# Six staging slots, later loads and projections dealt out over slots, in layers 2 and 3 of a four-layer block on one core

## The reference, cut to what matters

```
def layer2(x, c, context):                      # x: (4, 1024, 256), 16 heads of 16
    shift_a, scale_a, gate_a, shift_m, scale_m, gate_m = split(silu(c) @ W_mod + b_mod, 6)
    q, k, v = split((ln(x) * (1 + scale_a) + shift_a) @ W_qkv + b_qkv, 3)
    x = x + gate_a * (softmax(q k^T / 4) v @ W_proj + b_proj)
    x = x + (softmax(q_c k_c^T / 4) v_c @ W_cproj + b_cproj)   # k_c, v_c from 77 context rows
    return x + gate_m * (gelu((ln(x) * (1 + scale_m) + shift_m) @ W_mlp1 + b_mlp1) @ W_mlp2 + b_mlp2)

def layer3(x, context, c):
    return x + (softmax(q_3 k_3^T / 4) v_3 @ Wp + bp)
```

## Time and profile before

| | |
|---|---|
| median of 3 runs | 3452.23 us (3444.96 to 3454.8) |
| the profiled execution | 3451.98 us |
| its span, first to last instruction | 3450.2 us, mean granted TensorE clock 0.950 |
| TensorE busy (products) | 3162.4 us, 92% of the span |
| VectorE busy | 1824.0 us, 53% |
| ScalarE busy | 1467.0 us, 43% |
| GpSimd busy | 256.9 us, 7% |

### The profile page before, as it was taken

One profiled execution on the slowest core, in us unless ns is written; L12 is line 12 of the kernel. 1 busy time (PEld: TensorE's weight loads), 2 busy tenths in 40 slices (PEclk: granted clock), 3 DMA queues, 4 the chain that ended last, 5 costly groups with the idle time before them and its releaser, 6 DMA issues.

```text
span 3450.2 us, 52900 instructions
## 1 busy us (share of the span) xinstructions
PE 3162.4 (92%) x21156; PEld 1867.7 (54%) x21156; DVE 1824.0 (53%) x3812; ACT 1467.0 (43%) x2645; POOL 256.9 (7%) x278
## 2 busy tenths in 40 slices
PE   6899999999889999999389989999999999999987
PEld 3555665656566666666244445454454544554464
DVE  4876554563411322322278865757756577556433
ACT  0343535444322222221136645565455565565533
POOL 1100010001100000000100001001110101001010
PEclk9898999999898999999789999999999999999998
DMA  5200000002100000000321020001200000000000
GB/s 168 91 1 6 8 21 1 8 21 68 45 12 11 0 1 1 1 0 1 135 77 35 26 74 25 11 24 44 86 13 22 28 29 25 13 28 25 7 1 13
DMA packets 78713, 104.39 MB, mean 30 GB/s; under 512 B 18688, under 2 KB 52208, under 8 KB 78204
## 3 DMA queue, kind: packets, MB, share of 16 engines
q1 hardware_dynamic: 78468, 100.93, 8.9%
HBM read 72.05 MB, written 28.86 MB: 29 GB/s over the span
## 4 chain that ended last, share of the span: by engine, by line
PE 80%; DVE 10%; DMA 3%; ACT 3%; issue 2%; SPq 1%; POOL 1%; DVEq 0%; ACTq 0%; POOLq 0%
PE ps L978 73%; PE ps L1193 3%; DVE max_halves L1684 2%; DMA k_parts<-qk_parts 1%; PE ps L1320 1%; PE ps L1184 1%; DVE row_max_cross L1850 1%; DMA q_parts<-qk_parts 1%; PE ps L1172 1%; ACT big L2028 1%; ACT probs L2087 1%; DVE bn_stats L1720 1%; DMA q_blocks<-q_parts 1%; DVE xn_tok L1756 1%; SPq L879 1%
## 5 line engine op out<-in xcount | busy, mean ns | idle before, releaser
L2028 ACT ACTIVATE big<-ps 128x512 f32<-128x512 f32 x1280 | 693.7, 595 | 639.5 <-PE ps L978 638.6
L1684 DVE TENSOR_REDUCE max_halves<-ps 128x1 f32<-128x512 f32 x1024 | 650.4, 684 | 222.1 <-PE ps L978 219.4
L978 PE MATMUL ps<-k_groups,q_blocks 32*128 32x512 f32 x2048 | 451.6, 463 | 71.0 <-DVE qk_parts L1819 34.8
L978 PE MATMUL ps<-q_blocks,k_groups 32*128 32x512 f32 x2048 | 422.5, 466 | 3.3 <-DVE qk_parts L1819 2.0
L978 PE MATMUL ps<-big,probs 128*32 128x512 f32 (+2 forms) x3280 | 397.1, 531 | 5.0 <-ACT o_T L2003 3.8
L978 PE MATMUL ps<-weights_mlp,big 128*128 128x256 f32 (+1 forms) x1248 | 333.4, 419 | 2.5 <-ACT big L2099 2.5
L978 PEld LDWEIGHTS ps<-q_blocks,k_groups 32*128 32x128 f32 x2048 | 178.4, 185 | 286.1 <-issue 273.9
L978 PEld LDWEIGHTS ps<-weights_mlp,big 128*128 128x128 f32 x1248 | 233.7, 190 | 83.9 <-issue 58.0
L978 PEld LDWEIGHTS ps<-k_groups,q_blocks 32*128 32x128 f32 x2048 | 197.6, 189 | 120.9 <-DVE qk_parts L1819 39.0
L1726 DVE TENSOR_TENSOR x_tok<-ps,x_tok 128x512 f32<-128x512 f32 x112 | 77.3, 691 | 307.6 <-PE ps L978 307.4
L2087 ACT ACTIVATE probs<-ps 77x512 f32<-77x512 f32 x384 | 196.5, 592 | 96.8 <-PE ps L978 96.5
(11 more groups left out here) (233 smaller groups left out, 3913.6 us busy)
## 6 DMA issues: line engine op xcount, KB each, us to landing
q_blocks<-q_parts SPq DMA_DIRECT2D x64, 256.0 KB
q_parts<-qk_parts SPq DMA_DIRECT2D x48, 256.0 KB
k_parts<-qk_parts SPq DMA_DIRECT2D x32, 256.0 KB
k_groups<-k_parts SPq DMA_DIRECT2D x16, 512.0 KB
weights_mlp<-in_L_xcond_mlp_W SPq DMA_DIRECT2D x5, 1024.0 KB, 5.4
weights_mlp<-in_L_xcond_W_mlp SPq DMA_DIRECT2D x5, 1024.0 KB, 5.6
x_tok<-in_x SPq DMA_DIRECT2D x4, 1024.0 KB, 9.6
out_y<-x_tok SPq DMA_DIRECT2D x8, 512.0 KB, 2.9
```

The costliest lines, as they stand in the source:

```text
L978: return pe.matmul(out, lhsT, rhs, start=first, stop=last)
L1684: dve.tensor_reduce(NMP[:, e, j, qt, hf:hf + 1], PS[:, bank, :], AX.X, ALU.max, negate=True).then_inc(R.frees(key), 1)
L2028: act.activation(PB[:, score % 2, j, :], PS[:, R.bank(key), :], ACT.Exp, scale=SCALE).then_inc(R.frees(key), 1)
```

## The change: what it does

1. Item 0's staging gets four more slots (`EARLY`, in a part of `big` that cross-attention and the MLP use later). Projections 0 and 1 use the two old slots, 2 to 5 the four new ones, and from projection 6 on the two old slots alternate. Six semaphores count the writes. `parts_before(n)` is the projection whose writes n waits for: n - 6 for projections 6 and 7, n - 2 later.
2. `p_tokens` puts the v product of each half of the heads behind that half's four projections, not behind all eight.
3. `open_to` deals the projections out. Item 0's first four are free; its projections 4 to 7 wait for slots -8, -4, 0 and 4. Projection n of a later item b waits for slot 6 + 6n of item b - 1.
4. Item 0's loads are placed only when three block loads have been placed. SP issues the weights (W1, two biases, the four cross-attention weights) behind the third block load, and these four weights are taken into the same function.
5. Item 0's gates are placed 60 us after their loads on the planner's clock, not 14 us. The planner's estimate for a block load is 12 us for the first and 6 us for a later one, at least 3 us after the one before.

```diff
+        EARLY = BIG[:, 12288:16384].rearrange("p (s x n) -> p s x n", s=4, x=2)
+
+        def parts_at(n):
+            return EARLY[:, n - STAGES] if STAGES <= n < STAGES + 4 else STG[:, n % STAGES].bitcast(F32)
...
-                done = sum(48 if k[2] == 0 else 32 for k in self.parted[n % STAGES:n + 1:STAGES])
-                return self.part_out[n % STAGES], done
+                done = sum(48 if k[2] == 0 else 32 for k in self.parted[n % 6:n + 1:6])
+                return self.part_out[n % 6], done
+
+            def parts_before(self, n):
+
+                return self.parted[n - 6 if n < 6 + STAGES else n - STAGES]
...
-                return out + [("qk", b, m, a, hf) for m in range(KT) for a, hf in ((1, 0), (1, 1), (0, 0), (0, 1))] + [("v", b, m) for m in range(KT)]
+                for m in range(KT):
+                    out += [("qk", b, m, a, hf) for a, hf in ((1, 0), (1, 1), (0, 0), (0, 1))] + [("v", b, m)]
+                return out
...
-                    out.append((("gate", what, b), [("load", what, b)], 14.0))
+                    out.append((("gate", what, b), [("load", what, b)], 60.0 if R.split and not b else 14.0))
...
                 if kind == "qk" and R.split:
-                    return True
+                    n = 4 * tok[2] + (tok[4] if tok[3] else NH + tok[4])
+                    return t >= (tok[1] - 1) * R.total + 6 + 6 * n if tok[1] else n < 4 or t >= 4 * n - 24
...
-                    if item in loads and item[2] == 0.0 and all(k in ended for k in item[1]):
+                    if item in loads and item[2] == 0.0 and all(k in ended for k in item[1]) and (not R.split or state["ld"] >= Q_BLOCKS):
...
-                    ended["ld", state["ld"] - 1] = state["now"] + 5.0
+                    ended["ld", state["ld"] - 1] = max(state["now"] + (12.0 if state["ld"] == 1 else 6.0), ended.get(("ld", state["ld"] - 2), 0.0) + 3.0)
...
-            for item in list(loads):
+            for item in list(loads) if not R.split else ():
...
+                def weights():
+                    sp.dma_start(W1, rowsview(io[pre + ("mlp_W1" if R.l == 0 else "W_mlp1")])).then_inc(R.w1_in, 16)
+                    if R.l == 2:
+                        sp.dma_start(BX, bcast(io[L2 + "b_cproj"])).then_inc(R.w1_in, 16)
+                        sp.dma_start(B3, bcast(io[L3 + "bp"])).then_inc(R.w1_in, 16)
+                        sp.dma_start(Wcq, rowsview(io[L2 + "W_qc"])).then_inc(cross_w, 16)
...
+                if not R.split:
+                    weights()
...
+                    if tok == ("ld", Q_BLOCKS - 1):
+                        weights()
...
-                            if n >= STAGES:
-                                dve.wait_ge(*R.parts_landed(*R.parted[n - STAGES]))
+                            if n >= 6:
+                                dve.wait_ge(*R.parts_landed(*R.parts_before(n)))
...
-                            if n >= STAGES:
-                                act.wait_ge(*R.parts_landed(*R.parted[n - STAGES]))
-                            act.activation(STG[:, n % STAGES, 0, :], PS[:, R.bank(tok), 0:w], ACT.Identity, bias=QB[:, 3 * a, m:m + 1]).then_inc(R.part_hi, 1)
+                            if n >= 6:
+                                act.wait_ge(*R.parts_landed(*R.parts_before(n)))
+                            act.activation(parts_at(n)[:, 0, :].bitcast(F32R), PS[:, R.bank(tok), 0:w], ACT.Identity, bias=QB[:, 3 * a, m:m + 1]).then_inc(R.part_hi, 1)
```

More of the change, by code:

```diff
@@ L322, in __init__ @@
                     self.part_hi, self.nm_f, self.nm_h = sems(name, "part_hi max_f32 max_hi")
-                    self.part_out = sems(name, "parts_out_0 parts_out_1")
+                    self.part_out = sems(name, "parts_out_0 parts_out_1 parts_out_2 parts_out_3 parts_out_4 parts_out_5")
                     self.q_in = sems(name, "q_block_in_0 q_block_in_1 q_block_in_2")
@@ L689, in overlapped @@
                 for item in list(loads):
-                    if item in loads and all(k in ended for k in item[1]) and max(ended[k] for k in item[1]) + item[2] <= now:
+                    if item in loads and item[1] and all(k in ended for k in item[1]) and max(ended[k] for k in item[1]) + item[2] <= now:
                         loads.remove(item)
@@ L719, in overlapped @@
                 else:
-                    waits = [f[0] for f in found] + [max(ended[k] for k in item[1]) + item[2] for item in loads if all(k in ended for k in item[1])]
+                    waits = [f[0] for f in found] + [max(ended[k] for k in item[1]) + item[2] for item in loads if item[1] and all(k in ended for k in item[1])]
                     assert waits, (R.name, state, [s[h] for h, s in zip(heads, streams) if h < len(s)], loads)
@@ L860, in gate @@
                     sp.dma_start(dst, MODd[b:b + 1, base + chunk * D:base + (chunk + 1) * D].broadcast_to([P, D])).then_inc(done, 16)
[L862 to L865, removed]
+                def weights():
[4 more added lines that the diff above has]
+                        sp.dma_start(Wcq, rowsview(io[L2 + "W_qc"])).then_inc(cross_w, 16)
+                        sp.dma_start(Wco, rowsview(io[L2 + "W_cproj"])).then_inc(cross_w, 16)
+                        sp.dma_start(Wcq3, rowsview(io[L3 + "Wq"])).then_inc(cross_w, 16)
+                        sp.dma_start(Wco3, rowsview(io[L3 + "Wp"])).then_inc(cross_w, 16)
+                if not R.split:
+                    weights()
                 for tok in R.order:
@@ L878, in region_sp @@
                             dst = KPd[b, m, :, x, :, hf * HALF:(hf + 1) * HALF] if a else QPd[b, m, hf, :, x]
-                            sp.dma_start(dst, STG[:, n % STAGES, part, :].bitcast(F32)).then_inc(R.part_out[n % STAGES], 16)
+                            sp.dma_start(dst, parts_at(n)[:, part, :]).then_inc(R.part_out[n % 6], 16)
                     if tok[0] == "ld":
@@ L967, in _ @@
             sp.dma_start(BV, bcast(io[L2 + "b_qkv"][2 * D:3 * D])).then_inc(bv_in, 16)
[L968 to L971, removed]
             region_sp(L2R)
@@ L1813, in region_dve @@
                             n = R.parted.index(tok[1:])
-                            parts = STG[:, n % STAGES]
+                            parts = parts_at(n)
                             dve.wait_ge(*R.full(tok))
-                            if n >= STAGES:
-                                dve.wait_ge(*R.parts_landed(*R.parted[n - STAGES]))
+                            if n >= 6:
+                                dve.wait_ge(*R.parts_landed(*R.parts_before(n)))
                             dve.wait_ge(R.part_hi, n + 1)
-                            dve.scalar_tensor_tensor(parts[:, 1, :], PS[:, R.bank(tok), 0:w], QB[:, 3 * a, m:m + 1], parts[:, 0, :].bitcast(F32), ALU.add, ALU.subtract).then_inc(R.frees(tok), 1)
+                            dve.scalar_tensor_tensor(parts[:, 1, :].bitcast(F32R), PS[:, R.bank(tok), 0:w], QB[:, 3 * a, m:m + 1], parts[:, 0, :], ALU.add, ALU.subtract).then_inc(R.frees(tok), 1)
                         elif hf:
```

## The result

The changed kernel takes 3430.62 us (median of 4 runs, 3422.96 to 3432.92) and the kernel before, run beside it, 3453.52 us: 0.9938 of it, with an interval of [0.9917, 0.9959]. It is faster by 23 us, where 42 were forecast. The profiled execution took 3432.92 us, with a span of 3431.1 us.

The account below looks back on a forecast made before the run. A chain of write, landing, evacuation and bank bounds the start, TensorE the rest of layers 2 and 3. -49 + 10 - 6 + 2 + 1 = -42 from 3452 gives 3410 us, range 3396 to 3438.

Parts of the forecast that it names:

- first exponential: Start of layers 2 and 3: item 0's first exponential at 1720 us instead of 1769.05, -49 us.
- moved work: Four projections, a v pair and item 1's transposes move into slots bound by TensorE: net +10 us (8 to 13).
- gates: Item 0's gate products on POOL near slot 8, between two row-maximum steps: taken as +1 us, up to 8 if colliding.
- block loads: Item 0's slots: q writes ahead of block 8's load cost 3 us, block 4 gains 1.03: +2 us (0 to 12).
- dealing out: Items 1 to 3, a projection every six slots: waits in the two later clusters go, -6 us (0 to -12).
- estimate of about 4 us that stood beside the sum: Each block load behind a projection's three q writes pays about 4 us if both use the same four DMA engines.
- the 3 us that should have come back as waits: TensorE's waits for projections between 1764 and 1804.6 us lose their cause; 3 us counted as gain against moved work.
- Transfers did not bind the start: Rival, chance 0.15: at the start block 0 lands at 1694 us as before, block 1 is 10 us late; 3427 us.
- dealt projections were not dear: Rival, chance 0.10: a dealt-out projection holds a bank and costs 1 us more for each of 24; 3434 us.
- the change did what it says: Denies a rival, chance 0.05: ring full for another reason, block 0 no earlier, TensorE waits elsewhere; 3447 us.
- The rival of block loads: Rival, chance 0.05: dealt-out writes delay six block loads in item 0's slots, TensorE starves; slower from about 9 us each.
- waits for POOL's row maxima near slot 14 (gates): Sign that the forecast is wrong: in item 0's slots, the gates delay POOL's row maxima; no size given.

Follow-up runs that it names:

- later gates: The changed kernel with the planner's delay of item 0's gates at 90 us, not 60: 3411.85 us, 0.9885; again side by side 3417.16 us, 0.9912.
- mean of eight: The eight profiles of kernels with dealt projections and six staging slots: 1225.3 to 1232.1 us from slot 64 to the last exponential.
- three with clusters: The kernel before, and the changed kernel without dealing out items 1 to 3, gates' delay 90 us (3432.15 us, 0.9943) and 112 us (3421.84 us, 0.9927).
- the two comparisons of the changed kernel: The changed kernel timed against the kernel before twice: 3430.62 us, 0.9938; again, beside two other kernels, 3423.75 us, 0.9927.
- the last projection behind the load: The changed kernel with gates' delay 90 us and the eighth projection of items 1 to 3 two slots later: 3413.88 us, 0.9908; again 3414.03 us, 0.9903.

## Why the prediction was wrong in size

The mechanism of the start was right: write, landing, evacuation and bank bound it, and the change took that chain away. Of the five terms one was too small by a factor of ten or more, and two by some us. Measured from the traces named, of which the kernel before has one:

| term | forecast | measured | how |
|---|---|---|---|
| first exponential | -49 | -45 to -48.5 | v bias to it: 118.1 before; 69.6, 72.8 after, 69.7 to 72.9 in four profiles with later gates |
| moved work | +10 | +14 to +15 | slots 0 to 64 without the two collisions: 246.2 and 245.3, before 231.5 |
| gates | +1 | +10 to +14 | slots 0 to 64: 262.1 and 265.9, with later gates 252.4 and 251.6 |
| block loads | +2 | +6 | the same, 252.4 and 251.6 against 246.2 and 245.3 |
| dealing out | -6 | about -5, not settled | behind slot 64: mean of eight 1229.2, of three with clusters 1234.4; waits 43.7 and 48.9 |

With the middle of each row that is -47 + 14.5 + 12 + 6 - 5 = -19.5 us; the two comparisons of the changed kernel gave -23 and -24.

**The step that failed is the price of the gates**, "put near slot 8 it lies between two of POOL's row-maximum steps [...] I take 1". They do lie there, from 1745.2 to 1756.9 us, between row maxima at 1745 and 1787.7 us. What the step left out is the neighbour on another engine: the prediction looked for the wait in GpSimd's own queue, and in another term wrote that "DVE takes item 1's layer norm over into these slots", with 39 us free to cover it. The two were never laid beside each other in time. The trace of before had rows that price such a meeting, from an earlier layer, which the prediction did not use. In the kernel before, the single durations of VectorE's line (minimum, median, maximum in ns), then VectorE's and GpSimd's timelines at its longest:

```profile
L1756 DVE TENSOR_SCALAR xn_tok<-x_tok,mean_var,rstd x224: 381/407/4601, 95.7 to 3393.3; 128x256 f32<-128x256 f32 x112
```

```profile
904.04 5.98 DVE L1756 TENSOR_SCALAR xn_tok<-x_tok,mean_var,rstd 128x256 f32<-128x256 f32 x4 [0.49 <-POOL rstd L2244]
```

```profile
903.97 4.51 POOL L2209 TENSOR_TENSOR weights_mlp<-weights_mlp,gates_biases 128x2048 f32<-128x2048 f32 x1
```

Four normalisations that need 1.6 us took 5.98 us beside a product of the same shape. Two such products in a row make it 8 us, and as the transposes stand next in TensorE's list, that is 9.1 us of wait, with the granted clock near its lower level of 1.2 GHz around its end (0.53 from 1753 to 1764 us). The Trainium skill, SBUF — State Buffer, section "Who interferes with whom", says that a tensor_scalar of VectorE can run in a mode in which it needs the port pair that GpSimd uses, that the one that comes first then blocks the other for its whole instruction, and that a tensor_reduce never contends on this chip. The rows agree on both: normalisations that ended 0.15 us behind a product, and reductions at 0.683 us beside one. The ports themselves no run here shows. The prediction did not draw on that section.

**Block loads.** The place was forecast (block 8, three q writes ahead of it), the price was 3 us of wait less 1 us; the wait was 4.16 us, and with a granted clock of 0.77 from 1925 to 1940 us, in part at the lower level behind that wait, slots 48 to 64 lost 6 us. But the forecast's "only one load has q writes right ahead" was a misreading: block 5's load stood behind three q writes as well. SP's queue of the changed kernel:

```profile
1826.29 1.89 SPq L898 DMA_DIRECT2D q_parts<-qk_parts  x3
1828.28 3.07 SPq L912 DMA_DIRECT2D q_blocks<-q_parts  x2
```

TensorE did not wait for it (from slot 8 to 48 it waits only for ScalarE, 2.2 us). Block 5 loads no k group and so half the bytes of block 8; that this is the reason was not tested. The estimate of about 4 us that stood beside the sum, by the Trainium skill, DMA: Bandwidth & Descriptors, section "Why a DMA increments its semaphore by 16 and not by 1", fits the wait for block 8 (4.16 us, and 0.4 us with the writes behind the load), while for block 5 it cost TensorE nothing. On which engines a transfer ran no run here shows.

**Moved work.** TensorE's groups in slots 0 to 64 of the kernel before, and of the one with the last projection behind the load (projections, v, transposes; busy us, mean ns):

```profile
L978 PE MATMUL ps<-probs,weights 128*128 128x512 f32 x16 | 9.1, 720 | 0.0
...
L978 PE MATMUL ps<-weights,probs 128*128 128x128 f32 x32 | 3.8, 278 | 0.0
...
L1193 PE MATMUL ps<-ident,xn_tok 128*128 128x128 f32 x8 | 1.0, 272 | 0.0
```

```profile
L995 PE MATMUL ps<-probs,weights 128*128 128x512 f32 x36 | 17.4, 607 | 0.0
L995 PE MATMUL ps<-weights,probs 128*128 128x128 f32 x64 | 7.6, 277 | 0.0
...
L1210 PE MATMUL ps<-ident,xn_tok 128*128 128x128 f32 x24 | 3.9, 323 | 0.8 <-DVE max_halves L1701 0.8
```

A projection is four products, so five moved (8.3 us), not four; with v (3.8) and the transposes (2.9) that is 15.0 us, and the 3 us that should have come back as waits were taken up by others (TensorE is idle for 9.4 us of these slots before and 9.2 us here). A dealt projection itself takes about 1.9 us up to TensorE's next product (1781.44 to 1783.35 us in the changed kernel) against 1.74 forecast, and brings no wait with it: from slot 8 to 48 TensorE is idle for 2.2 of 142.7 us.

**The rivals.** Transfers did not bind the start (fills at 1684.4 us, not 1694), dealt projections were not dear, and the change did what it says. The rival of block loads happened at one load of six, and its sign was seen there (a wait for q blocks at slot 53). The true case was none of them: a wait between two engines that share no queue. The measured 3430.62 us lies between the 3427 and 3434 us of two rivals, neither of which happened: the time alone would have spoken for them. Of the signs named ahead, "waits for POOL's row maxima near slot 14 (gates)" looked at the wrong victim.

## What to carry to other kernels

When work is moved, lay it in time beside what every other engine does there, not only beside its own queue: an idle engine's product can stop a neighbour that has 39 us to spare, if the neighbour's instruction stands ahead of the bottleneck's next one. Before pricing such a meeting, look in the old trace for the longest single duration of each instruction, not its mean (here 4.60 us against a median of 0.41), and for what ran beside it. And a queue order by estimated times needs a check of the places that come out of it: delays of 14 and 60 us hit two different victims, 90 us hit none, and a change elsewhere moved the gates back.

## What the runs showed of the hardware

VectorE's normalisation from SBUF to SBUF (128x256, 0.40 us) took 3.86 and 4.58 us when it met GpSimd's products of 128x2048 (4.55 us), while VectorE's reductions from PSUM beside the same products stayed at 0.683 us, and GpSimd's products were no longer in either case (4.55 and 4.56 us). The whole cost fell on VectorE; GpSimd's product had started first each time, and the other order was not run.
